# Moving the output projection of a delta-rule attention kernel into the middle of the error products

## The reference

```python
def attn(x):                                   # H = 16 heads, d = 32
    rk = x.reshape(B, T, H, d); rk = rk / norm(rk)      # read key
    wk = rk shifted by one time step                    # write key
    v = (x @ Wv.T).reshape(B, T, H, d)
    gate, beta = sigmoid(x @ Wg.T), sigmoid(x @ Wb.T)
    for t in range(T):                         # S: d x d state of each head
        err = (v[t] - wk[t] @ S) * beta[t]
        S = S + outer(wk[t], err)
        o[t] = (rk[t] @ S) * gate[t]
    return o.reshape(B, T, D) @ Wo.T
x = x + layernorm(attn(layernorm(x)))
x = x + layernorm(ffn(layernorm(x)))           # ternary weights, clipped inputs
```

## Time and profile before

| | |
|---|---|
| median of 3 runs | 2370.92 us (2365.35 to 2374.8) |
| the profiled execution, its own time | 2373.69 us |
| span of its trace | 2372.0 us |
| mean granted TensorE clock | 0.966 |
| busy share of the span | PE 89%, DVE 84%, ACT 73%, POOL 73% |

### The profile page before, as it was taken

How to read it: one execution, slowest core, us unless ns; L and a number is a source line. 1 busy time by engine, 2 the same in 40 slices (tenths; PEclk the granted TensorE clock), 3 DMA queues, 4 the chain that set the end, 5 groups by cost and what they waited for, 6 DMA issues and landing times. The chain is left out here.

```text
span 2372.0 us, 145909 instructions
## 1 busy us (share of the span) xinstructions
PE 2108.6 (89%) x61992; PEld 1334.4 (56%) x61992; DVE 1985.7 (84%) x5810; ACT 1727.6 (73%) x3628; POOL 1726.7 (73%) x3098
## 2 busy tenths in 40 slices
PE   1679999999999999999999999999999988499997
PEld 1355666566666665656666656666666655255554
DVE  5487899888898888988898888989988985488886
ACT  3767777777777777777777777877777743477775
POOL 2667888888888888888888888888888853144343
PEclk7789999999999999999999999999999997799999
DMA  2111222222222222222222222222222211478885
GB/s 86 51 43 58 76 79 77 75 75 76 78 77 75 74 76 75 76 75 76 76 78 77 75 75 77 78 75 77 77 80 77 59 61 49 151 196 231 227 229 131
DMA packets 132139, 215.53 MB, mean 91 GB/s; under 512 B 31353, under 2 KB 31361, under 8 KB 131489
## 3 DMA queue, kind: packets, MB, share of 16 engines
q1 hardware_dynamic: 131488, 206.20, 30.0%
HBM read 104.40 MB, written 67.11 MB: 72 GB/s over the span
## 5 line engine op out<-in xcount | busy, mean ns | idle before, releaser
L775 DVE TENSOR_TENSOR ps_elim<-ps_elim,sys 128x30 f32<-128x30 f32 (+14 forms) x1920 | 543.6, 326 | 0.8
L783 DVE TENSOR_TENSOR sys<-sys,ps_elim 128x30 f32<-128x30 f32 (+14 forms) x1920 | 534.8, 316 | 1.0
L900 PE MATMUL ps_v<-wv,xt 128*128 128x512 f16 x1536 | 429.7, 390 | 26.1 <-DMA kbd<-kt 13.5
L900 PE MATMUL ps_y<-wo,ot 128*128 128x512 f16 x1536 | 406.9, 388 | 11.6 <-DVE x L827 9.5
L927 PEld LDWEIGHTS ps_chain<-rhs,t_t 32*32 32x32 f32 x16384 | 263.4, 144 | 132.9 <-issue 131.6
L927 PE MATMUL ps_chain<-rhs,t_t 32*32 32x32 f32 x16384 | 296.1, 218 | 24.3 <-issue 18.4
L684 ACT ACTIVATE state<-ps_s 128x512 f32<-128x512 f32 x128 | 76.5, 598 | 265.0 <-PE ps_s L991 265.0
L921 PEld LDWEIGHTS ps_chain<-state,key_t 32*32 32x32 f32 x16384 | 174.8, 105 | 152.6 <-issue 151.1
L991 PEld LDWEIGHTS ps_s<-err,key_b 32*32 32x32 f32 x16384 | 172.6, 107 | 142.9 <-issue 142.3
L1277 PE MATMUL ps_f<-wq,f_xq 128*128 128x512 f16 x1024 | 242.6, 381 | 6.7 <-DVE f_xq L1243 6.7
L803 DVE TENSOR_TENSOR rhs<-val,ps_chain 128x512 f32<-128x512 f32 x128 | 88.0, 687 | 188.3 <-PE ps_chain L921 187.7
(11 more groups left out here) (159 smaller groups left out, 5072.2 us busy)
## 6 DMA issues: line engine op xcount, KB each, us to landing
x_in<-in_L_attn_x SPq DMA_DIRECT2D x128, 256.0 KB
kbd<-kt SPq DMA_DIRECT2D x512, 64.0 KB, 2.0
x_res<-in_L_attn_x SPq DMA_DIRECT2D x128, 256.0 KB
x_scratch<-x SPq DMA_DIRECT2D x128, 256.0 KB, 6.4
f_x<-x_scratch SPq DMA_DIRECT2D x32, 1024.0 KB, 7.7
out<-f_res SPq DMA_DIRECT2D x128, 256.0 KB, 3.8
gate<-gates SPq DMA_DIRECT2D x128, 7.9 KB
gate<-gates SPq DMA_DIRECT2D x128, 0.2 KB
```

Of the source, the lines that this page charges most:

```text
L775: dve.tensor_tensor(tmp, factors(r, c, first, end)[:, c - first:C - 1 - first, c - first:c - first + 1].to_broadcast(shape), sys[:, r, c:c ...
L783: dve.tensor_tensor(dst, dst, tmp, ALU.add).then_inc(elim_done[r], 1)
L900: last = pe.matmul(out, lhs[:, a, kb, :], weights[:, w, kb, :], start=(i == 0), stop=(i == 3 * KB - 1))
```

## The change

PE's two waits for the output projection, and its first four products, stand around the second half of the error product; two products fewer are left for the end of the step. The number of instructions stays the same.

```diff
@@ PE's step, ahead of the error products
+                y, y_l, y_live = on(base, j, LAG_Y)
+
+                def output(first, end):
+                    if y_live:
+                        return project(ps_y[:, :], ot[:, y_l % 2], k["wo"], range(first, end))
+
                 value(2 * SHARE, 3 * SHARE - 1)
                 error_ready(base, j)
                 value(3 * SHARE - 1, 3 * SHARE)
                 solve_error(0)
                 last = value(3 * SHARE, 4 * SHARE)
                 if v_live:
                     last.then_inc(s["v_psum"], 1)
+                if y_live:
+                    wait(pe, s["x1_done"], y)
+                    wait(pe, s["ot_done"], y + 1)
+                output(0, 2)
                 last = solve_error(1)
                 if live:
                     last.then_inc(s["err_psum"], 1)
+                output(2, 4)
...
@@ behind the key transposition (SHARE is 3, WHOLE is 12)
-                if y_live:
-                    wait(pe, s["x1_done"], y)
-                    wait(pe, s["ot_done"], y + 1)
-                output(0, SHARE - 1)
+                output(4, 5)
                 update_ready(base, j)
-                output(SHARE - 1, SHARE)
+                output(5, 6)
                 update(0)
-                output(SHARE, 2 * SHARE)
+                output(6, 8)
                 last = update(1)
...
-                output(2 * SHARE, WHOLE - 1)
+                output(8, WHOLE - 1)
                 if y_live:
                     chain_ready(base, j + 1)
                 last = output(WHOLE - 1, WHOLE)
```

More of the change, by code:

```diff
@@ L979, in step @@
                     last.then_inc(s["kt_psum"], 1)
-                y, y_l, y_live = on(base, j, LAG_Y)
                 n, l, live = on(base, j, 0)
-                def output(first, end):
-                    if y_live:
-                        return project(ps_y[:, :], ot[:, y_l % 2], k["wo"], range(first, end))
                 def update(half):
```

## The result

| | median | runs |
|---|---|---|
| before | 2369.65 us | 4, 2365.35 to 2374.8 |
| changed | 2526.88 us | 4, 2522.08 to 2533.97 |

The ratio is 1.0665, with a 95% interval of 1.0631 to 1.0699: slower, by 157 us where 88 were forecast, and 12 us above the range that ended at 2515. The profiled execution took 2533.97 us.

A forecast was written before the change was run, and what follows sets the result against it. PE's instructions in order plus instruction-supply holes bound each step. 0.88 (x1 wait) + 0.10 (x_res) - 0.28 (given back) = 0.70 us a step, 83 us over 118 steps, tail 3: 2459 us; 8 in 10 from 2405 to 2515.

The forecast's parts named there:

- The clock row under 1.00: Sign of a wrong prediction: PE's granted clock, forecast to stay 1.00 in the changed kernel, falls below it.
- The wait for x1: Ahead of the second error half, PE waits for DVE's x1: 1.62 us even, 0.52 odd steps; 0.88 us a step left.
- What comes back (-0.28 us): Instruction-supply holes behind the new wait and at the prediction shrink: 0.13 and 0.15 us a step; bounds 0 and 0.86.
- its 70 to 90: Sign: PE's recorded issue holes in the groups shown should fall from 101 us to 70 to 90 us.
- The clock (0): PE's clock behind the new pauses: expected to stay 1.00, nothing in the sum; a fall was only a rival.
- A group's end (0): Extra time where small tiles follow an output group: taken as 0; 0.10 us a step, 12 us, if one more paid.
- x_res (0.10): SP's x_res load, issued 0.88 us nearer the next prediction, delays x1 in some odd steps: 0.10 us a step, bounds 0 and 0.44.
- kbd (free): SP's four kbd transfers come 0.88 us later, ahead of the gram product; more than 1.6 us of slack, no cost.
- State and error copies (free): State copy keeps 0.8 of 1.2 us slack before the prediction; error copy gains one product of cover; no cost.
- DVE's wait for the prediction: Sign: DVE's idle time until PE has predicted should grow from 158.7 to about 240 us.
- the supply: Rival: blocks arriving during PE's wait replace the holes, 2371 to 2388 us or faster, to 2354; chance 0.12, of it 0.03 faster.
- the clock rival: Rival: 1.6 us pauses halve PE's clock behind them, 1.5 us each even step, 88 us more, about 2547; chance 0.07.

The follow-up runs named there:

- the two runs without the wait: x1 reads a constant row instead of the projection, no wait for DVE: changed kernel's order 2376.63 us, order of the kernel before 2363.25 us.
- the run without the dependence: Changed kernel, but x1 reads a constant row instead of the projection and PE waits only for ACT's read of the bank: 2376.63 us, ratio 1.0006.
- the runs with shorter steps: The 11.7 us belongs to the changed kernel with waits and first four output products behind the second error half, 2396.62 us; the 8.3 us run isn't identified.
- x1 later: Changed kernel with x1 on DVE behind the second third of the elimination instead of ahead of it: 2930.01 us, ratio 1.2336.
- the run with fewer groups: Kernel before with prediction halves in a row, no values between gram and error, no output between update halves: 2414.93 us, ratio 1.0071.

## Why the prediction was wrong in size

Direction, place and main term were right. Two terms of the sum failed: the clock, put at nothing, and the time given back, put at -0.28 us a step. The clock row under 1.00 was among the prediction's own signs of being wrong, and it came.

- **The wait for x1**: right in place, cause and size. 0.88 us a step (0.98 with x_res) forecast, 0.96 measured from group to group and 0.87 as recorded wait. An even step waits 1.29 us on average (about 1.6 where no hole comes first), an odd one 0.50. One moved semaphore and DVE's order set it.
- **What comes back (-0.28 us)**: this term failed. The holes fell by only 0.09 us a step. With the waits alone moved they fell by 0.30, the forecast's size; but the new order costs holes at the prediction (L921: 40.6 against 30.4 us, and 50.4 against 34.1 in the two runs without the wait), where I had let half of them vanish. That the transfers of x cause these holes was my guess; no run showed it, and why the order brings them stays open. The recorded holes of the groups that the prediction added up are 84 us, inside its 70 to 90; but the stretch holds 109 steps instead of 118, so that most of the fall from 101 us is no gain.
- **The clock (0)**: I had it as a rival at 0.07 chance and 88 us, and counted nothing in the forecast. This is the largest part that the sum lacked. It took 0.34 us a step, 40 us: in 28 of 102 steps, nearly all of them behind a long pause, at 1.2 us a time. That PE kept 1.00 with holes in it was poor evidence: between 200 and 1850 us of that trace only two pauses of PE are over 1.25 us, the longest 1.33; the changed kernel has 47. Only about six in ten of its pauses of 1.25 us or more at the new place are followed by slow products; which are, stays open.
- **A group's end (0)**: it is 0.10 us, the bound that I named. I had supposed that products joined to a value group save an end. Without the wait they do (0.09 us, the run without the dependence); with it, x1 sets when the first of them starts, and what the value group saves only makes the pause longer.
- **x_res (0.10)**: right in kind, too large: x1 waited 5.5 us for it in all, 0.05 us a step, and 2.2 us before.
- **kbd (free)**: 2.4 us here, but 8.3 and 11.7 us in the runs with shorter steps. Its slack was read from one step.
- **A small slip**: by the earlier trace rows x1 starts 5.06 us behind rhs in the even step and 3.95 in the odd one, so it comes 1.1 us later, not 1.2. Nothing hangs on it.
- **State and error copies (free)**: right; PE never waits for them.
- **DVE's wait for the prediction** should have grown to 240 us; it stayed at 156.7. The growth went to an earlier instruction, the gates (134.8 us, before 32.2), which wait for their input from ACT. The step is no shorter for it.
- **The sum**: 0.96 + 0.34 + 0.10 - 0.09 in place of 0.88 + 0.10 - 0.28. The wait and the clock together make more than nine tenths of it.
- **Rivals**: the supply takes at most 0.30 us a step of the pause back (waits alone moved), and 0.15 of 2.21 us more of pause (x1 later); the clock rival was half right, since it falls in a quarter of the steps, not half.

## What to carry to other kernels

A wait moved forward on the engine that sets the step costs the distance between its new place and the time at which the other engine's instruction ends, both measured from the signal that starts that other engine; one error half of distance, 1.04 us, was worth 130 us here, clock included. Price the clock behind each new pause as a term of the sum. And don't credit holes of instruction supply against a wait before a run has shown that they go.

## What the runs showed of the hardware

The granted clock fell behind pauses of 1.3 to 1.7 us in an otherwise busy step, for a few groups of instructions, and four fillers of 0.21 us inside the pause mostly kept it up. Between 200 and 1850 us the traces have this many stretches at the half clock: none before, 29 in the changed kernel, 32 with the waits alone moved, 3 without the dependence, 6 with the fillers, 82 with x1 later. PE's holes of instruction supply change when the order does: without any wait for x1, those at the prediction were 50.4 us in the new order and 34.1 in the old. And an order with fewer group ends can be the slower one, as the run with fewer groups was.
